# Delta rule: one product a level carries the factor beside the inverse, VectorE turns it and ScalarE copies both

## The reference, cut to what matters

```python
def step(S, inp):
    q_t, k_t, v_t, g_t, b_t = inp
    Sk = jnp.einsum('bhkv,bhk->bhv', S, k_t)
    delta = jnp.einsum('bhv,bhk->bhkv', v_t, k_t) - jnp.einsum('bhv,bhk->bhkv', Sk, k_t)
    S = jnp.exp(g_t)[..., None, None] * S + b_t[..., None, None] * delta
    o_t = jnp.einsum('bhkv,bhk->bhv', S, q_t)
    return (S, o_t)
```

## Time and profile before

| | |
|---|---|
| median of 3 runs | 4261.81 us (4256.46 to 4264.55) |
| profiled execution | 4283.9 us, its span 4282.1 us |
| TensorE busy | 3885.2 us (91%), 51725 matmuls |
| VectorE busy | 3064.9 us (72%), 5127 instructions |
| ScalarE busy | 2237.7 us (52%), 3389 instructions |
| GpSimd busy | 1036.7 us (24%), 1042 instructions |
| TensorE's granted clock over the span | 0.966 of full speed |

### The profile page before, as it was taken

How to read it: one execution, slowest core, us unless ns; L and a number is a source line. 1 busy time by engine, 2 the same in 40 slices (tenths; PEclk the granted TensorE clock), 3 DMA queues, 4 the chain that set the end, 5 groups by cost and what they waited for, 6 DMA issues and landing times. The chain is left out here.

```text
span 4282.1 us, 127123 instructions
## 1 busy us (share of the span) xinstructions
PE 3885.2 (91%) x51725; PEld 2324.9 (54%) x51725; DVE 3064.9 (72%) x5127; ACT 2237.7 (52%) x3389; POOL 1036.7 (24%) x1042
## 2 busy tenths in 40 slices
PE   5999778888888888897887999999999999999998
PEld 4444367777778777675663344444444444444443
DVE  5799856555555555444896787878878787878786
ACT  2788734444444444233442565656656565656564
POOL 1000055555555555102777000000000000000000
PEclk9999999999999999998896999999999999999999
DMA  3544432222222222224345000000000000000000
GB/s 126 183 124 124 142 116 81 84 79 89 85 83 79 85 82 83 75 86 142 106 110 121 8 5 19 5 8 15 10 15 10 13 5 20 5 20 3 10 15 10
DMA packets 271801, 265.25 MB, mean 62 GB/s; under 512 B 53760, under 2 KB 232064, under 8 KB 270496
## 3 DMA queue, kind: packets, MB, share of 16 engines
q1 hardware_dynamic: 250768, 226.07, 17.7%
q0 software_dynamic: 6144, 16.79, 1.2%
q10 hardware_dynamic: 14352, 14.55, 1.0%
HBM read 151.95 MB, written 105.38 MB: 60 GB/s over the span
## 5 line engine op out<-in xcount | busy, mean ns | idle before, releaser
L2418 DVE TENSOR_REDUCE part_max<-p_m 128x1 f32<-128x512 f32 x2118 | 1363.9, 686 | 378.1 <-PE p_m L2260 370.7
L2400 ACT ACTIVATE prob<-p_s 128x1024 f32<-128x1024 f32 x1024 | 1048.6, 1024 | 747.6 <-PE p_s L2324 745.6
L2279 PE MATMUL p_o<-prob,v_one 128*64 128x512 f32 x4096 | 1054.3, 592 | 3.9 <-ACT prob L2400 0.5
L2260 PE MATMUL p_m<-keys,queries 96*64 96x512 f16 x4236 | 661.4, 387 | 28.1 <-DMA keys<-parts_d 20.5
L2324 PE MATMUL p_s<-queries,keys 97*64 97x512 f16 x4096 | 619.0, 380 | 0.0
L2324 PEld LDWEIGHTS p_s<-queries,keys 97*64 97x64 f16 x4096 | 228.1, 109 | 598.4 <-issue 593.3
L2228 POOL TENSOR_TENSOR attn<-o_num,o_inv 32x512 f32<-32x512 f32 x64 | 81.2, 1268 | 1451.6 <-DVE o_inv L2437 1445.2
L852 PE MATMUL pd_pre<-inv_low,upper 64*64 64x64 f32 x10240 | 374.2, 222 | 45.3 <-issue 33.5
L2260 PEld LDWEIGHTS p_m<-keys,queries 96*64 96x64 f16 x4236 | 238.7, 108 | 311.1 <-DVE part_max L2418 56.5
L852 PE MATMUL pd_low<-inv,step 64*64 64x64 f32 x8192 | 365.1, 237 | 45.6 <-issue 42.2
L1143 ACT ACTIVATE inv<-pd_low 128x512 f32<-128x512 f32 x192 | 114.7, 598 | 519.1 <-DVE inv_low L1259 518.7
(11 more groups left out here) (236 smaller groups left out, 5777.7 us busy)
## 6 DMA issues: line engine op xcount, KB each, us to landing
q_d<-conv_q SPq DMA_DIRECT2D x16, 1024.0 KB, 5.0
v_d<-conv_v SPq DMA_DIRECT2D x16, 1024.0 KB, 5.0
k_d<-conv_k SPq DMA_DIRECT2D x16, 1024.0 KB, 6.5
sums<-sums_d SPq DMA_DIRECT2D x128, 128.0 KB, 3.1
kq_t<-k_d SPq DMA_DIRECT2D x32, 512.0 KB, 3.7
kq_t<-q_d SPq DMA_DIRECT2D x32, 512.0 KB, 4.8
sums_k<-sums_d SPq DMA_DIRECT2D x128, 128.0 KB
v_t<-v_d SPq DMA_DIRECT2D x32, 512.0 KB
```

What stands on the lines that cost most here:

```text
L2260: last = te.matmul(p_m[k % 2][x * HALF:(x + 1) * HALF, :], queries[0:ROW, p, hh, at:at + HALF], keys[0:ROW, 2 * p + hh, kb * BLK:(kb + 1) ...
L2279: product = te.matmul(p_o[64 * hh:64 * hh + VW, :], g.v_one[:, j, p, hh:hh + 2, :].rearrange("p a d -> p (a d)"), prob[:, j % 2, hh, :], s ...
L2400: a.activation(prob[:, j % 2], p_s[j % 2][:], ACT.Exp, scale=SCORE_SCALE).then_inc(exp_d, 1)
L2418: v.tensor_reduce(part_max[:, hh * SUB + sub, kb:kb + 1], p_m[k % 2][:], AX.X, ALU.max).then_inc(red_d, 1)
```

## The change

For each chunk the changed kernel keeps the factor inv(U-I) beside the inverse. Both lie in one tile, `both` [128, 8, 128], the factor in columns 0 to 63 and the inverse in 64 to 127, and in one pair of PSUM banks, `p_both`. A start product (`start_factor`, 64 columns) makes the first factor. At each of the levels 1 to 4 one product of 128 columns (`double`) multiplies both by the same step. VectorE then turns the factor half out of the bank (`turn`), and makes the next step from the turned tile by a mask (`mask`), whose two inputs both lie in SBUF. ScalarE copies both halves (`keep_both`, 1024 wide) after VectorE has read the bank. At the fifth level the step is a block of the turned factor that ScalarE copies with its sign changed (`last_step`), into a tile whose other blocks GpSimd fills once; only the inverse is multiplied (64 columns). A 128 wide product takes two 64 wide ones of the other kind beside it (`long_beside_short`). The key rows of chunk 1 move into the next iteration. `upper` has one buffer for each chunk where it had two.

```diff
-    p_pre = [ps(f"pd_pre{x}") for x in range(2)]
-    p_low = [ps(f"pd_low{x}") for x in range(2)]
+    p_both = [ps(f"pd_both{x}", 2) for x in range(2)]
...
+        def start_factor(n, x):
+            return lambda p, h: te.matmul(p_both[x][half_of(h), p, 0:C], inv_low[x][half_of(h), p, :], upper[x][half_of(h), p, :],
+                                          start=True, stop=True)
...
+        def double(n, x, k):
+            if k < NL:
+                return lambda p, h: te.matmul(p_both[x][half_of(h), p, :], step[x][half_of(h), p, :], both[x][half_of(h), p, :], start=True, stop=True)
+            return lambda p, h: te.matmul(p_both[x][half_of(h), p, C:2 * C], step_last[x][half_of(h), p, :], inv_half[x][half_of(h), p, :],
+                                          start=True, stop=True)
...
+        def long_beside_short(long, short):
+
+            for p in range(NPAIR):
+                for h in range(2):
+                    a = long(p, h)
+                    if p < NPAIR // 2:
+                        for hh in range(2):
+                            b = short(2 * p + h, hh)
+            return a, b
...
+            wait_double(pre, 1, 1)
+            wait_key_rows(post, 1)
+            made, turned_keys = long_beside_short(double(pre, 1, 1), key_rows(post, 1))
+            made.then_inc(upmm_d[1], 1)
+            turned_keys.then_inc(kr_d[1], 1)
...
-        def keep_inverse(n, x, k):
-            act.wait_ge(upmm_d[x], n.level[k])
-            if k < NL:
-                act.wait_ge(lowc_d[x], n.level[k + 1])
-            a.activation(inv_half[x][:] if k == NL - 1 else inv[x][:], p_low[x][:], ACT.Copy).then_inc(up_d[x], 1)
...
+        def keep_both(n, x, k):
+            act.wait_ge(turn_d[x], n.level[k + 1])
+            a.activation(both[x][:], p_both[x][:], ACT.Copy).then_inc(up_d[x], 1)
...
+        def last_step(n, x):
+            act.wait_ge(turn_d[x], n.level[NL])
+            for h in range(2):
+                last = a.activation(step_last[x][h * C + B32:(h + 1) * C, :, 0:B32], turned[x][h * C:h * C + B32, :, B32:C], ACT.Copy, scale=-1.0)
+            last.then_inc(last_d[x], 1)
...
+        def turn(n, x, k):
+            dve.wait_ge(upmm_d[x], n.made[k])
+            if k == 1:
+                dve.wait_ge(last_d[x], n.last)
+            v.transpose(turned[x][:], p_both[x][:, :, 0:C]).then_inc(turn_d[x], 1)
+
+        def mask(n, x, k):
+            dve.wait_ge(turn_d[x], n.level[k])
+            v.tensor_tensor(step[x][:], turned[x][:], over_pairs(masks[:, k - 1, :]), ALU.mult).then_inc(step_d[x], 1)
```

More of the change, by code:

```diff
@@ L1097, in one @@
[L1097 to L1106 removed]
+                wait_updates(n, x)
@@ L1387, in one @@
             if ahead is not None:
-                for x in range(2):
-                    decays(ahead, x)
+                decays(ahead, 0)
+            if pre is not None:
+                grow_keys(pre, 0)
+            if ahead is not None:
                 scale_rel(ahead, 0)
```

419 lines of the change are left out of this document (208 added, 211 removed).

## The result

The changed kernel takes 4140.18 us (median of 4 runs, 4138.47 to 4151.36) where the kernel before takes 4260.16 (median of 4, 4256.46 to 4264.55). The ratio is 0.9724, with an interval of 0.9707 to 0.974: it is faster by 120 us. Forecast were 4225 us and at best 4168. The direction is right. The time lies three times as far from before as the forecast has it, and outside the range from 4168 to 4296.

What follows compares the result with a forecast made beforehand. TensorE was taken to bound the delta rule stage, by products, code and scatter. Terms -1.2 + 0.3 - 3.3 + 2.4 + 0.8 = -1.0 us a couple, with the prologue -37 us, gave 4225 us; 8 in 10 range 4168 to 4296.

Steps and rivals of the forecast that it cites:

- the scatter: TensorE slowed while GpSimd issues its two indirect DMAs: 1.5 us a couple, 0.7 of it inside "issue".
- the clock: Delta rule stage at granted clock 0.96, 8% of it at the lower level: some 1.2 us a couple.
- Products, -1.2 and +0.3: TensorE's products, fewer and wider: 1.2 us a couple less; short records beside long ones add 0.3.
- Code, -3.3: TensorE's waits for instruction packets: fewer matmuls at a slower rate leave 0.9 of 4.2 us a couple.
- Masks, +0.8: VectorE's eight masks a couple, now read from SBUF: 0.19 us longer each, half on the path, +0.8 us a couple.
- Waits, +2.4: TensorE's waits for transposes and copies between levels and at the couple's end: 5.6 against 3.2 us a couple.
- The level behind `grown`: Level 3 of chunk 0: ScalarE's copy queues behind `grown`, which waits for GpSimd's decay of the state: 2.0 us.
- Prologue, -6: Prologue, where products have no partner: one product a level instead of two, -6 us in all.
- larger gain: Rival, chance 0.2: masks aren't held and waits fill times in which code arrives; -93 us, 4169 us.
- Slower by held masks: Rival, chance 0.2: VectorE's masks and GpSimd hold each other in the first two levels; +31 us, 4293 us.
- Each packet halts as long as now: Rival, chance 0.05: each packet still halts TensorE 0.48 us, so 3.2 us a couple stay; 4296 us.
- no change: Rival, chance 0.1: the gain in code and the loss by waits on TensorE cancel; about 4258 us.

Runs made afterwards that it cites:

- a_split: The changed kernel with each doubling of levels 1 to 4 as two matmuls of 64 columns instead of one of 128: 4355.27 us, ratio 1.0158.
- b_light: The kernel before with loads of keys, queries and values cut to one pair of heads of eight from couple 2 on: 4199.33 us, ratio 0.9853.
- a_mask_one_input: The changed kernel with its eight masks a couple replaced by a transpose with one SBUF input: 4158.70 us, ratio 0.9698.
- a_grown_later: The changed kernel with ScalarE's grown(pre, 1) moved behind keep_both(pre, 1, 2): 4145.25 us, ratio 0.9724.
- a_values_mask: The changed kernel with grown(pre, 1) later, chunk 0's values turned and copied in mid-couple, and masks replaced by a one-input transpose: 4103.45 us, ratio 0.9626.

## Why the prediction was wrong

The direction and the mechanism of the gain hold. The size doesn't, and the step that failed is in "What bounds the kernel now" and the sum drawn from it: **the scatter** (1.5 us a couple, of which 0.8 was kept under waits and 0.7 taken out of what shorter code could give) and **the clock** (1.2 us, for which the sum has no term) were booked as costs of their own, which the change would leave. They went with the code instead: shorter code took them to 0.4 and 0.0, and a_split brought them back in part (37 us beside the scatter, a clock of 0.97). With these two at their measured size the sum would give 37.1 - 2.3 = 34.8 us a couple. The second miss, 1.8 us the same way, is the term for waits and masks. Point by point, in us a couple:

- *Products, -1.2 and +0.3.* Right: without all gaps a couple of the changed kernel takes 33.1 - (13 + 118 + 38) / 31 = 27.7 us, and 27.9 were foretold.
- *Code, -3.3.* Right in mechanism, as a_split shows by undoing it alone and the landings of the packets show directly, and nearly in what it leaves: 0.9 foretold, 38 / 31 = 1.2 measured. But it started from too little. Wandering gaps were 159 / 31 = 5.1 us a couple, not 4.2; a part of the "waits and restarts" was code too. The Trainium skill (Runtime: NRT & Kernel Launch, "Instruction fetch mechanics") calls the crossing of a 16 KiB block mostly hidden. Here it was not: a_split adds 63 packets to the same arithmetic, and 4.5% to the time.
- *Scatter, stays.* Wrong. Excess beside it fell from 50 us to 13, 1.6 to 0.4 a couple. Taking the scatter out of the kernel before gained nothing, so the lost progress was no price in time as long as packets were short. What makes the gaps stays open.
- *Clock, 0 change.* Wrong. The lower clock went with TensorE's halts: of the stage of the changed kernel only the first 2 us lie in it. b_light is the control, with the same instructions, shorter halts and a clock of 1.00.
- *Masks, +0.8.* The duration was forecast right (0.75 to 0.95 foretold, 0.96 measured), the share on the path wrong: 0.2 to 0.3% of the time at most in this kernel, intervals overlapping, against 25 us foretold. With one input the waits at fixed places fell by 24 us, the 25 foretold, but little of it reached the time. With the end shortened they cost 0.5.
- *Waits, +2.4.* Too much: 4.8 foretold without the scatter, 118 / 31 = 3.8 measured; in the kernel before 34 / 31 = 1.1 (more by the wider count of gaps), so the added part is up to 2.7. Of the items, the end (0.9) is confirmed by its removal, 24 / 31 = 0.8. The level behind `grown` (2.0) shows as a gap of 1.2 us in the timeline, and its removal gave nothing, for the reason above.
- *Prologue, -6.* Wrong in sign: 5.7 longer. The term counted a product less a level and left out the copies: ScalarE's take 1.02 us where they took 0.60, and with no other product to fill the wait they stand in the chain; the clock is 0.85 there where it was 0.95. That these two make the difference is argued, no run tests it. What comes behind the stage is 2.6 longer and wasn't forecast.

Put together, in us a couple:

| | forecast for after | measured |
|---|---|---|
| products and pace | 27.9 | 27.7 (the rest) |
| waits in the order | 4.8 | 3.8 |
| masks held | 0.8 | within the waits |
| halts for code | 0.9 | 1.2 |
| beside the scatter | 1.5 | 0.4 |
| lower clock | 1.2 | 0.0 |
| sum | 37.1 | 33.1 |

The 4.0 us between them are scatter 1.1, clock 1.2, masks and waits 1.8 and products 0.2, less 0.3 for code. Seen from before, the wandering gaps, the scatter's and the clock came to 5.1 + 1.6 + 1.2 = 7.9 us a couple, and the prediction gave the change only 4.2 of them to work on. That is the step that failed.

Of the rivals, "larger gain" (4169) named the right side; its reason, that waits fill times in which code arrives, is half of what the table shows, and its other one, masks not held, is false. "Slower by held masks" is refuted by the result and by a_mask_one_input: the masks do get longer (0.96), the path hardly feels it. "Each packet halts as long as now" is refuted: 159 us became 38 while packets went from 272 to 209. The sentence under "no change", that what one shortage frees the other may take, holds in the waits taken away from the changed kernel: nearly all came back in a_grown_later, half in a_values_mask. Of the signs named beforehand, records (43533), copies (1.02), packets (209) and waits on VectorE and ScalarE (54.7) came as foretold; the masks' mean of 0.96 is a hair over the forecast's 0.95; "issue" stayed at 67.5 us, above the 50 foretold, while only 38 wander.

Open: what makes the gaps beside the scatter, which come after every few records and not at a border, and why shorter code has fewer of them; how many and which halts bring the clock down; what made the prologue longer; and why the profiled execution of before lies 24 us above the median of its runs.

## What to carry to other kernels

Where a stage of small matmuls shows much idle time on "issue", count its instructions against the packets of the instruction queue before looking for waits, and sort its gaps into those that come at the same place of each iteration and those that wander; better still, look whether its halts end at a fixed time after a packet landed. One wide matmul in place of two narrow ones is then worth more than its work, and a low clock or a slow stretch isn't booked as a cost of its own before asking whether it would exist without the shortage. The other way round, a wait taken away from an engine that is short of code gives back only a part: here half of 101 us.

## What the hardware showed that was not expected

- TensorE's halts for code end 1.20 to 1.60 us after an instruction packet landed: 83 of 88 halts over 0.7 us in the kernel before, 31 of 113 in the changed one, where most of the gaps come at the same place of each couple.
- The place of a shortage moves. With the scatter removed, 50 us of gaps disappeared beside it and 77 appeared elsewhere (up to 30 of them the chip's), with a time of 0.9994 (0.998 to 1.0008).
- Light DMA loads in place of full ones, with the same instructions, took the longest halts from 3.2 to 1.8 us, the clock from 0.96 to 1.00, and 1.5% off the time.
- Going from 848 to 976 to 1104 records a couple adds 2.0% and then 2.3% to the time, with the same arithmetic.
- A VectorE mask with two SBUF inputs goes up to 1.52 us from 0.69 while GpSimd works, and GpSimd's operation from 1.18 to 1.51. The time of the kernel feels it by 0.4% at most.
